# Four large transfers for sixteen small ones in an attention block, with keys in another partition order and strided projection reads

## What is computed

```
x = x + attn(layernorm(x))        # 16 heads of 64, causal, softmax over keys
x = x + ffn(layernorm(x))         # 352 hidden units
attn: q, k, v = x Wq + bq, x Wk + bk, x Wv + bv
      p = softmax(mask(q k^T / 8));  out = (p v) Wo + bo
ffn:  h = silu(fp4(x) fp4(Wg)^T) * (fp4(x) fp4(Wu)^T);  out = fp4(h) fp4(Wd)^T
```

## Time and profile before

| what | us |
|---|---|
| median of 3 runs (lowest, highest) | 1229.36 (1229.16, 1230.98) |
| the profiled execution | 1228.53 |
| its span, first to last instruction | 1226.8 |
| PE, DVE, ACT, POOL busy | 1195.1, 1114.9, 990.3, 876.1 |
| mean granted clock of TensorE (share of 2.4 GHz) | 0.994 |

### The profile page before, as it was taken

One profiled execution on the slowest core, in us unless ns is written; L12 is line 12 of the kernel. 1 busy time (PEld: TensorE's weight loads), 2 busy tenths in 40 slices (PEclk: granted clock), 3 DMA queues, 4 the chain that ended last, 5 costly groups with the idle time before them and its releaser, 6 DMA issues. The chain is left out here.

```text
span 1226.8 us, 37232 instructions
## 1 busy us (share of the span) xinstructions
PE 1195.1 (97%) x10428; PEld 913.0 (74%) x10428; DVE 1114.9 (91%) x3722; ACT 990.3 (81%) x2878; POOL 876.1 (71%) x1389
## 2 busy tenths in 40 slices
PE   7899999999999999999999999999999999999877
PEld 5577777777777777777777777777777777777666
DVE  5797999999999999999999999999999999999967
ACT  6888898888888888888888888798888888888621
POOL 2575667778777787777788777777867778777761
PEclk9999999999999999999999999999999999999989
DMA  5576656566555656555565665666656565666630
GB/s 106 138 182 168 174 151 162 152 162 168 152 154 146 169 148 175 151 155 160 142 174 148 164 162 146 154 156 162 167 149 161 140 166 156 156 156 153 160 81 22
DMA packets 132525, 185.58 MB, mean 151 GB/s; under 512 B 40200, under 2 KB 66784, under 8 KB 132320
## 3 DMA queue, kind: packets, MB, share of 16 engines
q1 hardware_dynamic: 82128, 98.99, 31.3%
q10 hardware_dynamic: 50192, 84.21, 26.5%
HBM read 11.10 MB, written 4.19 MB: 12 GB/s over the span
## 5 line engine op out<-in xcount | busy, mean ns | idle before, releaser
L599 POOL TENSOR_SCALAR sc<-sc,rinv 128x128 f32<-128x128 f32 (+3 forms) x1024 | 537.0, 542 | 292.9 <-DVE rinv L1081 289.7
L762 ACT ACTIVATE sc<-sc,negmax 128x384 f32<-128x384 f32 (+3 forms) x1024 | 562.8, 552 | 157.5 <-DVE negmax L1070 114.8
L1070 DVE CUSTOM_DVE_ANT_0 sc<-bank,mask 128x512 f32<-128x512 f32 (+3 forms) x1024 | 436.6, 485 | 71.0 <-issue 53.1
L251 PE MATMUL bank<-k_sb,q_sb 64*128 64x512 f32 (+3 forms) x2048 | 314.7, 444 | 5.5 <-ACT k_sb L783 2.5
L267 PE MATMUL bank<-pT,v 128*64 128x128 f32 x5120 | 309.9, 276 | 8.1 <-DMA pT<-squares 5.3
L267 PEld LDWEIGHTS bank<-pT,v 128*64 128x64 f32 x5120 | 279.0, 137 | 50.6 <-issue 45.8
L251 PEld LDWEIGHTS bank<-k_sb,q_sb 64*128 64x128 f32 x2048 | 167.6, 187 | 142.2 <-issue 100.3
L1091 DVE STREAM_TRANSPOSE squares<-sc 128x1024 f32<-128x1024 f32 (+1 forms) x192 | 194.7, 1042 | 4.7 <-DMA pT<-squares 2.2
L1091 DVE STREAM_TRANSPOSE w_in<-sc 128x1024 f32<-128x1024 f32 (+1 forms) x192 | 192.2, 1039 | 1.8 <-POOL sc L599 1.6
L762 ACT ACTIVATION_READ_ACCUMULATOR sc<-sc,negmax 128x1 f32 x1024 | 193.6, 189 | 0.0
L374 PEld LDWEIGHTS bank<-wo_sb,zT 128*128 128x128 f32 x1024 | 131.2, 192 | 9.8 <-issue 0.7
(11 more groups left out here) (131 smaller groups left out, 1670.9 us busy)
## 6 DMA issues: line engine op xcount, KB each, us to landing
pT<-squares ACTq DMA_DIRECT2D x512, 80.0 KB, 2.3
pT<-squares SPq DMA_DIRECT2D x512, 80.0 KB, 2.4
pT<-w_in SPq DMA_DIRECT2D x512, 80.0 KB, 2.5
pT<-w_in ACTq DMA_DIRECT2D x512, 80.0 KB, 2.5
x_in<-ttn_normalized_resid_pre SPq DMA_DIRECT2D x16, 256.0 KB, 3.6
x<-ttn_normalized_resid_pre SPq DMA_DIRECT2D x16, 256.0 KB, 3.1
out_x<-y_out SPq DMA_DIRECT2D x32, 128.0 KB, 2.5
w_in<-in_L_attn_Ks SPq DMA_DIRECT2D x2, 256.0 KB, 5.0
```

The lines of the kernel that those rows point to most:

```text
L251: last = nc.tensor.matmul(to[a][:, at:at + m], q_sb[rows, hs % 2, P * i:P * i + P], k_sb[rows, hs % 2, 0:m], start=True, stop=True)
L599: last = nc.gpsimd.tensor_scalar(p, p, rinv[:, h % 2, a, i:i + 1], 1.0, ALU.mult, ALU.mult)
L762: last = nc.scalar.activation(p, p, ACT.Exp, scale=-1.0, bias=negmax[:, he % 2, a, i:i + 1], accum_out=rsum[:, he % 2, a, i:i + 1])
L1070: last = nc.vector.tensor_tensor_reduce(out=sc[:, h % 2, a, AT[i]:AT[i] + m], in0=bank_at[f"S{c}{a}", h][:, at:at + m], in1=mask[:, SEQ - ...
```

## The change

- The 16 moves of a pair become four, all issued by SP: transfer g takes 32 partitions of `squares` with all four c (10,240 bytes a partition) and writes all 128 partitions of `pT` (2,560 bytes each). Partition 4 k + c of `pT` now holds key 32 c + k, where it was partition 32 c + k. ScalarE's `move` and its 40 calls are gone; nothing else in ScalarE's order changes.
- So that the values have the same order of keys, x is loaded with row 128 j + 32 c + k in partition 4 k + c, as four transfers a batch (one per j) instead of one.
- The columns of x_hi and x_lo follow that order. `vproj` reads them as before; `project` reads them through a rearranged view (j, c, k) whose innermost step is four elements, 16 bytes, so that queries and keys come out in the natural order.
- The semaphore counts follow. One `warm_end(7)` of the tail becomes `warm_end(13)`, and an increment of a counter that nobody waits for (`passed`) goes.

```diff
+    xk = x.rearrange("b (j c k) d -> b j k c d", c=4, k=32)
@@ values
-                    pe.wait_ge(p_moved[pv % 2][c], 4 * 16 * (pv // 2 + 1))
+                    pe.wait_ge(p_moved[pv % 2][c], 16 * (pv // 2 + 1))
@@ project
-                       [v[:, pb % 2, :] for v in (x_hi, x_lo)]).then_inc((q_done, k_done)[n], 1)
+                       [v[:, pb % 2, :].rearrange("p (j k c) -> p j c k", j=NT, c=4) for v in (x_hi, x_lo)]).then_inc((q_done, k_done)[n], 1)
@@ TensorE's tail, before hq_turn(28)
-            warm_end(7)
+            warm_end(13)
@@ load (SP)
-                    src = xv[b]
                     if b > 1:
                         sp.wait_ge(x_normed, b - 1)
-                    sp.sem_inc(passed, 1)
-                    sp.dma_start(x_in[:, b % 2, :, :], src).then_inc(x_loaded[b % 2], 16)
+                    for j in range(NT):
+                        sp.dma_start(x_in[:, b % 2, j, :], xk[b][j]).then_inc(x_loaded[b % 2], 16)
@@ moves (SP)
-                for d in range(2):
-                    for c in range(4):
-                        g = (c + d) % 4
-                        sp.dma_start(pT[32 * c:32 * c + 32, h % 2, g, :, :],
-                                     squares[h % 2][32 * g:32 * g + 32, c, :, :]).then_inc(p_moved[h % 2][c], 16)
+                for g in range(4):
+                    sp.dma_start(pT[:, h % 2, g, :, :],
+                                 squares[h % 2][32 * g:32 * g + 32, :, :, :]).then_inc(p_moved[h % 2][g], 16)
@@ ScalarE
-            def move(hm, c, d):
-                for n in range(3):
-                    act.wait_ge(p_turned[n], hm + 1)
-                if hm > 1:
-                    act.wait_ge(z_done, hm - 1)
-                g = (c + d) % 4
-                act.dma_start(pT[32 * c:32 * c + 32, hm % 2, g, :, :],
-                              squares[hm % 2][32 * g:32 * g + 32, c, :, :]).then_inc(p_moved[hm % 2][c], 16)
@@ ScalarE's loop, and likewise in its first calls and its tail
-                move(pair(t + 20), 1, 2)
-                move(pair(t + 20), 0, 2)
-                move(pair(t + 20), 2, 3)
                 exp(pair(t + 22), 0, 1)
                 exp(pair(t + 22), 0, 0)
-                move(pair(t + 20), 1, 3)
...
@@ turn (VectorE)
-                        dve.wait_ge(p_moved[ht % 2][n], 4 * 16 * (ht // 2))
+                        dve.wait_ge(p_moved[ht % 2][n], 16 * (ht // 2))
@@ x_stat (VectorE)
-                dve.wait_ge(x_loaded[b1 % 2], 16 * (b1 // 2 + 1))
+                dve.wait_ge(x_loaded[b1 % 2], 16 * NT * (b1 // 2 + 1))
```

More of the change, by code:

```diff
@@ L870, in f_norm @@
                 last.then_inc(f_normed, 1)
-            def move(hm, c, d):
-                if hm is None:
-                    return
-                for n in range(3):
-                    act.wait_ge(p_turned[n], hm + 1)
-                if hm > 1:
-                    act.wait_ge(z_done, hm - 1)
-                g = (c + d) % 4
-                act.dma_start(pT[32 * c:32 * c + 32, hm % 2, g, :, :],
-                              squares[hm % 2][32 * g:32 * g + 32, c, :, :]).then_inc(p_moved[hm % 2][c], 16)
             def first(n):
@@ L936, in _ @@
             take_v(2)
-            move(0, 2, 2)
-            move(0, 0, 3)
             keys(3)
@@ L943, in _ @@
             exp(1, 1, 0)
-            move(0, 3, 3)
             exp(2, 1, 1)
@@ L947, in _ @@
             take_v(3)
-            move(0, 1, 3)
             exp(2, 0, 1)
@@ L954, in _ @@
             exp(3, 0, 1)
-            move(1, 2, 2)
             take_v(5)
-            move(0, 1, 2)
             keys(4)
             exp(3, 0, 0)
-            move(0, 2, 3)
-            move(0, 0, 2)
-            move(1, 0, 2)
             take_v(6)
-            move(0, 3, 2)
             exp(3, 2, 1)
@@ L967, in _ @@
             exp(3, 1, 0)
-            move(1, 1, 2)
-            move(1, 3, 3)
-            move(1, 2, 3)
             keys(5)
             exp(3, 1, 1)
-            move(1, 1, 3)
             take_v(8)
@@ L976, in _ @@
             queries(5)
-            move(1, 3, 2)
-            move(1, 0, 3)
             take_z(0)
@@ L981, in _ @@
                 take_weights(once(t + 10))
-                move(pair(t + 20), 1, 2)
-                move(pair(t + 20), 0, 2)
-                move(pair(t + 20), 2, 3)
                 exp(pair(t + 22), 0, 1)
                 exp(pair(t + 22), 0, 0)
-                move(pair(t + 20), 1, 3)
                 exp(pair(t + 22), 1, 0)
-                move(pair(t + 20), 2, 2)
                 exp(pair(t + 22), 2, 0)
-                move(pair(t + 20), 3, 2)
                 tanh(duo(t + 5), 0)
@@ L995, in _ @@
                 tanh(duo(t + 5), 1)
-                move(pair(t + 20), 0, 3)
                 take_x(batch(t + 29))
@@ L999, in _ @@
                 keys(pair(t + 24))
-                move(pair(t + 20), 3, 3)
                 f_norm(duo(t + 9))
@@ L1006, in _ @@
                 x_norm(batch(t + 30))
-            move(126, 0, 3)
             take_xq(28)
-            move(126, 0, 2)
-            move(126, 3, 3)
-            move(126, 2, 2)
             take_z(125)
[L1013 to L1016, removed]
             tanh(28, 0)
-            move(127, 2, 3)
-            move(127, 3, 3)
             f_norm(29)
-            move(127, 3, 2)
             tanh(28, 1)
[L1023 to L1027, removed]
             take_z(126)
```

## The result

The changed kernel takes 1387.2 us, median of four runs (1386.9 to 1388.1), against 1229.3 for the kernel before: a ratio of 1.129, with a 95% interval of 1.127 to 1.130. The profiled execution has a span of 1385.3 us, 158.5 more than before.

What follows compares the result with a forecast made beforehand. TensorE's queue was taken as the bound in the middle 1100 us. Strided read 153.6, start +0.5 and tail -5.5 gave +148.6 on 1228.5, so 1377.1, or 1378 as median; range 1219 to 1405.

Steps and rivals of the forecast that it cites:

- the likeliest case: Whole kernel: strided projection matmuls run at half rate, 1378 us, own range 1362 to 1405; chance 0.56.
- The bound: Middle 1100 us: TensorE's queue is the bound, so time added to a matmul lengthens the kernel one for one.
- The strided read: 768 query and key projection matmuls: 0.435 us instead of 0.235, +153.6 us, ends 0 and +288.
- The rule on 16-byte lines: Projections' moving reads: full speed needs at least two accesses per 16-byte line; one per line pays a penalty of unstated size.
- The moves: Mid-kernel: SP's four issues take 0.6 to 0.9 us each, last landing after 5 to 9 us, hidden; worth nothing.
- The start: First loads on SP, eight for two: what is queued behind comes 2.7 us later; net +0.5 us, bounds -2 and +3.
- The tail: Last pairs: pair 127's values could start 7.6 us earlier, feed-forward gains less; -5.5 us, between -3.4 and -7.6.
- A: Projections: the stride costs nothing, leaving the moves alone; 1224 us, from 1219 to 1231; chance 0.30.
- B: Projections: the stride costs more than half the rate, as by VectorE's pace, 0.61 us for 512 elements; 1512 us; chance 0.05.
- C: Moves: the four large transfers are slow, each reading only 32 partitions; 1354 us with free strides; chance 0.03.

## Why the prediction was right, and where not

The forecast was 1378 us and the time is 1387.2, inside the likeliest case's own range.

- **The bound.** Right: what was added to TensorE's matmuls came out one for one between the ends. A pair's two projections grew from 0.81 + 0.77 to 1.45 + 1.43 us, 1.30 in all, and 122 pairs lie between the first values and the last scores: 158.6 us, where 159.4 were measured.
- **The strided read.** Right in place and kind, undersized: a pitch of 0.46 us for a forecast 0.435. Two matmuls of three gained 0.225 us and the first of each three 0.19, 0.215 on average instead of 0.20. The forecast took the pitch at a clock of 1.2 GHz as the price of half the rate. For the earlier trace rows itself the profile has no clock record (the first begins at 17.7 us), but the row at 37.26, at 0.50, has the same 0.42 to 0.43. At that clock a strided matmul takes 0.46 too, so the read has a pace of its own that the row does not show, and that the two lie so near each other is in part luck. The term was 153.6 us; alone it measured 162.8. The reason given, that neighbours are fetched together, was half of it: pairs of neighbours are not enough here.
- **The rule on 16-byte lines** (the Trainium skill, Advanced Engine Details and Errata, section SBUF Cachelines). Its penalty exists, 0.46 us for 0.235. Its condition of two accesses on a line holds for the float32 stream (0.32 for 0.30) and fails for the float32r one (0.45 for 0.235), where four were needed.
- **The moves.** Hidden in mid-kernel, as forecast. The size of their issue was wrong: 1.27 us of SP's queue each, not 0.6 to 0.9. With 5.8 us from issue to landing the last one lands 9.4 us after the first issue, where 5 to 9 were given; the values start late enough to cover it.
- **The start.** The key weights were issued at 6.13 instead of 2.02, 4.1 us later where 2.7 were forecast; one load of 64 KB took 0.645 us, not 0.46. The first normalisation moved by 2.45, inside the +2.7. Up to the first values the changed kernel lost 4.1 us, the strided projections included; without the stride it lost 1.3 (49.47 against 48.19), where the forecast had 0.5.
- **The tail.** Forecast -5.5, measured -5.0, but by another split, and that is luck. Pair 127 was to land 6.8 us after SP's first issue, its values to start 7.6 us earlier, and the feed-forward chain to follow only in part. The values came 9.9 us after that issue for 14.5 before, 4.6 earlier, and not within 9; from there to the end both kernels took 43.2 us, so all of it was passed on. What holds them is the four issues and the landing: in the run with the moves alone they waited 2.06 us for the last move and came 10.3 us after the first issue. In that run's profile the start gave +1.3 us, the tail -4.3 and what lies between -1.0, for a forecast of -5.0 at the two ends.
- **The rivals.** A, the free stride, lost; its time of 1224 is what the moves alone gave (1224.0), so the sum of its other terms was sound, though not each of them. B named 0.61 us, which no float32r order reached. C did not happen: the four moves take 60.8% of sixteen engines, not twice the former time, although more than before, 842 us for 709 (60.8% of 1385.3 against 31.3 and 26.5% of 1226.8).

## What to carry over

Where TensorE is the bound, cost a new access pattern on its moving operand as you would an instruction: a step that only looks like addressing nearly doubled the pitch of 768 matmuls and outweighed nearly forty times what it made possible (162.8 us against 4.3). A permutation belongs on an engine with room: ScalarE's evacuation did it for nothing, reading PSUM with the step and writing SBUF in order. With it the four large moves are worth 0.25 to 0.65% here, depending on the form of the copy and the place of the loads; that the order of the moves is part of this is not shown.

## What the runs showed of the hardware

- A float32r moving operand needs the four elements of a 16-byte line within a few reads: 0.24 us for 512 columns, 0.46 in long strided runs, in between (0.26 to 0.33) where up to four lines are read in turn.
- A float32 one goes on with two elements of a line (0.32 for 0.30) and doubles with one (0.61 to 0.69); the scores' sixteen matmuls went from 2.36 to 4.68 us.
- The strided float32r pitch was 0.46 us at both clock levels, where the pitch in order went from 0.235 to 0.43; it is not set by TensorE's clock alone.
- ScalarE: 128 x 512 out of PSUM, 664 ns with reads 16 bytes apart, 1187 with writes to SBUF 128 bytes apart.
- A transfer of 320 KB from 32 to 128 partitions cost the DMA engines more than four of 80 KB from 32 to 32, all other traffic included: 842 and 836 us of sixteen engines with the large ones (60.8% of 1385.3, 68.4% of 1222.8), 709 and 722 with the small ones (57.8% of 1226.8, 52.0% of 1388.6). Size and target changed together; which of them costs is open.
- Issuing the four in the order 0, 2, 1, 3, which alternates between the lower and the upper 64 partitions, won back part of it, 840 to 770 us (68.8% of 1220.6, 63.2% of 1218.5).
